# Fusing the four activation transposes of a pair of batches into one piece of a hand-ordered TensorE schedule

## The reference

```python
q = (layernorm(x) @ Wq)                    # 32 x 112 x 256 -> 16 heads of 64
k, v = split(ctx @ Wkv)                    # 32 x 375 x 192 -> 16 heads of 64
x = x + softmax(q k^T / 8) v @ Wproj + bproj
# FFN: 8 experts, top 2 of softmax(h @ gate_w), h = layernorm(x)
x = x + sum_over_top2(prob * (silu(h @ gate) * (h @ up)) @ down)
```

## Time and profile before

| what | value |
|---|---|
| median of three runs | 1473.92 us (1473.84 to 1474.1) |
| the profiled execution's time | 1469.35 us |
| its span | 1467.6 us |
| PE busy | 1426.4 us (97%), 11960 matmuls |
| PEld busy (weight loads) | 1264.4 us (86%) |
| DVE busy | 1054.7 us (72%) |
| ACT busy | 854.5 us (58%) |
| POOL busy | 624.9 us (43%) |
| mean granted TensorE clock | 0.994 |

### The profile page before, as it was taken

The page is one execution under the profiler, slowest core; times in us unless marked ns, Lnnn a source line. Parts: engine busy times, 40 slices in busy tenths (PEclk is TensorE's granted clock), DMA queues, the critical chain, the costliest instruction groups (busy, mean ns, idle before and its releaser), DMA issues.

```text
span 1467.6 us, 38599 instructions
## 1 busy us (share of the span) xinstructions
PE 1426.4 (97%) x11960; PEld 1264.4 (86%) x11961; DVE 1054.7 (72%) x2868; ACT 854.5 (58%) x2392; POOL 624.9 (43%) x671
## 2 busy tenths in 40 slices
PE   6999999999999999999999999999997999999996
PEld 5888889888888888888888898888886788888885
DVE  5667777777777777777777777777767776666664
ACT  5566556555665566656655656566555565555553
POOL 3634344344545343544344444545436243333332
PEclk9999999999999999999999999999999999999999
DMA  9322222222222232322222222212128243333232
GB/s 264 108 68 69 75 72 76 67 76 67 73 67 75 72 88 76 99 74 67 73 67 77 70 73 70 73 38 73 31 64 312 50 69 54 57 51 57 51 57 26
DMA packets 101508, 114.75 MB, mean 78 GB/s; under 512 B 17276, under 2 KB 88172, under 8 KB 101356
## 3 DMA queue, kind: packets, MB, share of 16 engines
q1 hardware_dynamic: 88300, 95.25, 22.3%
q0 software_dynamic: 12144, 15.66, 6.0%
q10 hardware_dynamic: 1024, 3.34, 0.7%
HBM read 62.28 MB, written 51.93 MB: 78 GB/s over the span
## 4 chain that ended last, share of the span: by engine, by line
PE 91%; DVE 3%; DMA 3%; issue 1%; ACT 0%; ACTq 0%; POOLq 0%; DVEq 0%; SPq 0%
PE bank L1486 26%; PE bank L1429 21%; PE bank L1555 11%; PE bank L1531 10%; PE bank L1521 9%; PE bank L1576 6%; PE bank L1493 4%; DMA out<-y_out,dest_now 2%; PE bank L1729 2%; DVE probT L1285 1%; PE bank L1682 1%; DVE Wgu L1138 1%; DMA WkU_whole<-in_L_xattn_Wkv 1%; DVE stat L1127 0%; DVE x L1125 0%
## 5 line engine op out<-in xcount | busy, mean ns | idle before, releaser
L891 ACT ACTIVATE prob<-bank,neg_max 112x375 f32<-112x375 f32 x512 | 300.4, 589 | 136.1 <-DVE neg_max L1279 136.1
L1279 DVE TENSOR_REDUCE neg_max<-bank 112x1 f32<-112x375 f32 x512 | 243.8, 539 | 16.4 <-PE bank L1521 16.3
L1531 PE MATMUL bank<-ident,prob 112*125 112x112 f32 x1536 | 213.8, 273 | 2.6 <-ACT prob L891 2.4
L1531 PEld LDWEIGHTS bank<-ident,prob 112*125 112x125 f32 x1536 | 198.3, 188 | 16.1 <-ACT prob L891 4.7
L1555 PEld LDWEIGHTS bank<-probT,V 125*64 125x64 f32 x3072 | 149.0, 137 | 39.7 <-issue 37.0
L822 POOL DMA_INDIRECT out<-y_out,dest_now x63 | 97.8, 1552 | 199.9 <-DMA out<-y_out,dest_now 139.8
L1046 DVE TENSOR_TENSOR K_l<-bank,K_h 128x376 fp32r<-128x376 f32 x256 | 140.3, 549 | 57.1 <-ACT K_h L847 52.7
L1555 PE MATMUL bank<-probT,V 125*64 125x112 f32 x3072 | 176.6, 264 | 3.3 <-DVE probT L1285 2.5
L1429 PE MATMUL bank<-Wgu,hT_h 128*128 x504 | 164.7, 408 | 3.4 <-DVE hT_l L1347 2.8
L845 ACT COPY V<-bank 125x512 f32<-125x512 f32 x96 | 56.4, 587 | 164.7 <-PE bank L1493 162.2
L847 ACT CAST K_h<-bank 128x376 fp32r<-128x376 f32 x256 | 121.0, 473 | 31.2 <-PE bank L1486 29.7
(11 more groups left out here) (217 smaller groups left out, 3962.1 us busy)
## 6 DMA issues: line engine op xcount, KB each, us to landing
bins<-pad_rows SPq DMA_DIRECT2D x29, 1032.0 KB, 6.0
inv_rows<-sums SPq DMA_DIRECT2D x126, 128.0 KB, 2.9
h_in<-bins SPq DMA_DIRECT2D x63, 129.0 KB, 2.2
Wgu<-in_L_ffn_gate_up_w SPq DMA_DIRECT2D x6, 1024.0 KB, 6.8
y_sb<-in_ctx SPq DMA_DIRECT2D x32, 187.5 KB, 2.7
y_sb<-in_ctx SPq DMA_DIRECT2D x62, 93.8 KB, 2.7
x_sb<-in_x SPq DMA_DIRECT2D x16, 224.0 KB, 2.9
x_res<-in_x SPq DMA_DIRECT2D x32, 112.0 KB, 2.5
```

Of the source, the lines that this page charges most:

```text
L891: nc.scalar.activation(prob[:, j, :], S_ps[j][0:LQ, 0:LKV], ACT.Exp, bias=neg_max[:, j:j + 1], accum_out=row_sum[:, head // HB, head % HB: ...
L1279: nc.vector.tensor_reduce(neg_max[:, j:j + 1], S_ps[j][0:LQ, 0:LKV], AX.X, ALU.max, negate=True).then_inc(max_done, 1)
L1531: last = nc.tensor.transpose(S_ps[j][0:KR, t * LQ:t * LQ + LQ], prob[:, j, t * KR:t * KR + KR], ident[0:LQ, 0:LQ])
```

## The change

`xT` becomes one piece with four transposes, which fill 448 columns of one bank, one cast of 448 columns and one subtraction of 448 columns. It stands in "early" of the even batch's step 3. In that batch's step 2, q 7 goes from "mid" (bank `A_ps[0]`) to "late" (bank `A_ps[1]`), where `xT` 0 had been, and "mid" is empty. The odd batch's step 2 keeps q 2 in "mid" and q 3 in "late". In `START` one `xT` piece takes the place of two; it waits for both rows of `xn`. GpSimd's wait before it overwrites `xn` names the one piece.

```diff
     q_at = {(1, 0): (0,), (1, 1): (1,), (1, 2): (2, 3), (1, 3): (4,), (0, 0): (5,), (0, 1): (6,), (0, 2): (7,)}.get((odd, s), ())
-    one = [("q", p) for p in q_at] + {(0, 2): [("xT", 0)], (0, 3): [("xT", 1)]}.get((odd, s), [])
+    one = [("q", p) for p in q_at] + {(0, 3): [("xT", 0)]}.get((odd, s), [])
     places = {"K": [("K", 2 * s), ("K", 2 * s + 1)],
               "early": one if s != 2 else [],
-              "mid": one[:1] if s == 2 else [],
+              "mid": one[:-1] if s == 2 else [],
...
-              "late": one[1:] if s == 2 else []}
+              "late": one[-1:] if s == 2 else []}
...
-    ("K", 0), ("xT", 0), ("xT", 1), ("K", 1), ("K", 2), ("K", 3), ("q", 0), ("q", 1), ("K", 4), ("K", 5), ("q", 2),
+    ("K", 0), ("xT", 0), ("K", 1), ("K", 2), ("K", 3), ("q", 0), ("q", 1), ("K", 4), ("K", 5), ("q", 2),
...
-                    pool.wait_ge(made, a.made(a.find(int(a.first), "xT", 1)))
+                    pool.wait_ge(made, a.made(a.find(int(a.first), "xT", 0)))
...
-                    nc.scalar.copy(xT_h[:, :, arg * LQ:arg * LQ + LQ],
-                                   src[:, 0:2 * LQ].rearrange("p (k q) -> p k q", k=2)).then_inc(hi_done, 1)
+                    nc.scalar.copy(xT_h[:].rearrange("p k q -> p (k q)"), src[:, 0:4 * LQ]).then_inc(hi_done, 1)
...
-                    lo, hi = xT_l[:, :, arg * LQ:arg * LQ + LQ], xT_h[:, :, arg * LQ:arg * LQ + LQ]
-                    ps = src[:, 0:2 * LQ].rearrange("p (k q) -> p k q", k=2)
+                    lo, hi = [t[:].rearrange("p k q -> p (k q)") for t in (xT_l, xT_h)]
+                    ps = src[:, 0:4 * LQ]
...
-                    pe.wait_ge(xn_done, 2 * (0 if a.first else pair + 1) + arg + 1)
-                    for t in range(2):
-                        last = nc.tensor.transpose(dst[:, t * LQ:t * LQ + LQ], xn[:, arg, t * P:t * P + P],
-                                                   ident[0:LQ, 0:LQ])
+                    pe.wait_ge(xn_done, 2 * (0 if a.first else pair + 1) + 2)
+                    for r in range(2):
+                        for t in range(2):
+                            last = nc.tensor.transpose(dst[:, (2 * t + r) * LQ:(2 * t + r) * LQ + LQ],
+                                                       xn[:, r, t * P:t * P + P], ident[0:LQ, 0:LQ])
                 elif kind == "q":
                     if arg == 0:
-                        pe.wait_ge(lo_done, a.split(a.find(1 if a.first else 0, "xT", 1)))
+                        pe.wait_ge(lo_done, a.split(a.find(1 if a.first else 0, "xT", 0)))
```

## The result

The kernel before took 1474.05 us in the median of 22 runs (1471.9 to 1477.17), the changed kernel 1476.68 us in the median of 22 (1473.98 to 1481.01). The ratio is 1.002, with a 95% interval of 1.0013 to 1.0027: slower, by about the 0.2% that the forecast named. Two further comparisons of the same two kernels gave 1.0025 (1.0014 to 1.0037) and 1.0017 (1.0008 to 1.0026). The medians lie 2.63, 3.98 and 3.03 us apart in the three.

The account below looks back on a forecast made before the run. TensorE holds 91% of the chain, so the waits ending last in steps 2 and 3 decide. 15 x 0.19 = 2.8, + 0.2 + 0.15 = +3.15 us on 1473.92 gives 1477.1 us; range 1474.0 to 1479.2.

Parts of the forecast that it names:

- Step 3's wide cast: Even batch's step 3: the 448-column cast delays head 3's exponential, which its transposes wait for; +0.19 us a pair.
- The cover of 0.19: Even step 3: the existing 0.19 us wait for head 1's exponential absorbs two more transposes (+0.20), leaving +0.01.
- Rival 1: Even step 3: the wider cast is hidden, only 0.01 a pair and 0.35 us remain; 1474.4 us, chance 0.13.
- Step 2's two transposes: Even batch's step 2: removing two transposes (0.20 us) gains 0, since `weigh` waits for VectorE's two copies.
- Rivals 2 and 3: VectorE doesn't hold step 2's `weigh`: with step 3's loss 1472.3 us, chance 0.07; without it 1469.5 us, chance 0.04.
- The wide subtraction: Even step 3: the 448-column subtraction ends before the second V piece needs the bank, margin 0.27 us; cost 0.
- Rival 4: Even step 3: the wide subtraction makes the second V piece wait; 1478.7 us, chance 0.14.
- q 7 to "late": Even step 2: the same six products moved later, ready before step 3's `scores` with margin 0.8 us; cost 0.
- Batch 0: Step 2 of the first batch, without `project`: q 7 delays `weigh`; +0.15 us once, bounds 0 and 0.2.
- Start: Before the first pair: one four-transpose piece waits for both rows of `xn`; +0.2 us, bounds 0 and +0.24.
- A pair of 69.2: Changed profile: one pair of batches lasts 69.2 us, against 69.03 before.
- The rule on grouping: Skill page: grouping pays on a saturated engine, splitting may help otherwise; ScalarE, 41.62 of 69.03 us busy, put under the second.

Follow-up runs that it names:

- a_third: The changed kernel, unaltered, profiled a third time: 1473.54 us against 1470.51 for the kernel before, ratio 1.0017.
- a_stats_late: The changed kernel with VectorE's statistics of the residual moved behind its two copies in step 2: 1467.84 us, ratio 0.9984 to the kernel before.
- b_again: The kernel before, unaltered, run once more for a second profile: 1477.52 us in one run.
- a_again: The changed kernel, unaltered, run once more: 1476.24 us against 1472.26 for the kernel before, ratio 1.0025.
- a_narrow_cast: The changed kernel with ScalarE casting only the first 224 of 448 `xT` columns within the pairs: 1474.43 us, ratio 1.0012 to the kernel before.
- a_narrow_sub: The changed kernel with VectorE subtracting only the first 224 of 448 `xT` columns within the pairs: 1473.66 us, ratio 1.0011 to the kernel before.
- b_late_sums: The kernel before plus one VectorE operation of 224 columns ahead of the even step 3's inverse sums: 1471.54 us against 1469.74, ratio 1.0009.
- b_third: The kernel before, unaltered, profiled a third time: 1472.65 us in one run.

## Why the prediction was right, step by step

**The sum.** Forecast +3.15, 1477.1 us. Measured 1476.68, a difference of the medians of 2.63 (0.13% to 0.27% by the interval). The mechanism is the one forecast, with a size for each term. That the sum came out so close is in part luck: the three comparisons scatter from 2.63 to 3.98, batch 0 cost 0.12 more than its term, and the term for the start can't be told from the spread of one kernel's starts.

**Step 3's wide cast, +0.19 a pair.** Right: 0.179, 0.184 and 0.191 in three profiles, gone with a narrow cast. The spacing of 0.41 is the forecast's. Head 3's loads follow head 2's after 0.74 and not 0.79: over the fourteen pairs of a_third head 3's come 0.19 later than before, measured from `weigh` of step 2, but head 2's come 0.04 later too, where the forecast had 0.01 for head 1 and nothing for head 2. The cover of 0.19 for the two additional transposes held too: with the narrow cast they cost -0.004. Rival 1 (the cast is hidden) falls.

**Step 2's two transposes, 0.** Right: -0.013 to 0.003. Rivals 2 and 3 said that VectorE isn't what holds `weigh`. a_stats_late shows that it is: with VectorE out of the way the same two transposes and the wait are worth 0.314, where the forecast's rows gave 0.32.

**The wide subtraction, 0.** Right: it ended 0.28 before the V piece needed the bank, 0.27 was forecast, and making it narrow left step 3 as it was. Rival 4 falls.

**q 7 to "late", 0.** Right within the pairs. **Batch 0, +0.15:** mis-sized. It was +0.27, beyond its bounds of 0 and 0.2. Appending q 7 to the end of the transposes was right: its first load comes 6.81 after step 1's `weigh` (46.84 to 53.65), the old kernel's `xT` loads came 6.81 after it too (46.37 to 53.18), and the six loads take the forecast's 0.67. What was too small is the step from q 7 to `weigh`: I had allowed 53.85 to 53.95, but `weigh` starts 0.20 later than q 7's own spacing would have it (0.31 instead of 0.11). The profile names no releaser for these 0.20, and their cause stays open.

**Start, +0.2:** not to be resolved. The first scores came at 30.81, 34.56 and 30.47 with the kernel before, at 31.29, 34.88 and 31.76 with the changed one. Taken two by two that is +0.48, +0.32 and +1.29, but the spread of one kernel is 4 us. Nearly all of that spread goes with the moment at which TensorE's pace doubles (last section). An estimate from the fourteen executions, a straight line by that moment with one step for the new order, puts the new order's start 0.19 later, give or take 0.15, which neither contradicts nor proves the term.

**A pair of 69.2:** right in a_third (69.226), 0.2 short in the first profile (69.436). The difference isn't the change's: b_again shows the same +0.21 with the kernel before. I had carried one profiled execution to the median as if executions differed by a constant; they differ in the pairs too.

**The rule on grouping.** The rows first: ScalarE was 60% busy, two casts made one left its busy time at 41.62, and TensorE lost 0.19 a pair. The Trainium skill's page "Perfetto Trace Analysis" (section "Optimizing Scalar/DVE Operations") advises to break up instructions of an engine that isn't saturated but makes others wait; by that rule the trace agrees with the forecast's side. The prediction's remark that the change would pay by the first half of the rule was a slip: that half speaks of a saturated engine, which ScalarE is not.

## What to carry to other kernels

Grouping two small operations of an engine that isn't the bound saved nothing here, and it moved the next instruction in that engine's queue back by the added columns (0.19 us for 224): put the grouped piece where that next instruction isn't what TensorE waits for. Before work is taken off the busiest engine, look at who ends the wait at the next meeting point; if it is another engine's queue, as here the statistics ahead of two copies, reorder that queue first, and the saving appears (0.314 a pair). And where two profiles of the same kernel haven't been compared, a difference of 0.2 us a pair may be the execution's.

## What the runs showed of the hardware

**A pause behind step 3.** In five of the fourteen profiled executions (the changed kernel's first, b_again, a_again, a_narrow_cast, a_narrow_sub) the signals of TensorE's products reach the other engines late in the even step 3. The signal of `weigh`'s last product comes 0.28 us after the product's start in the nine others, and 0.81 to 0.95 in four of these five (0.66 to 0.73 in a_narrow_sub), in each of the pairs 1 to 14. It is late in the odd step 3 as well (0.54 to 0.67), where the pair gets no longer by it: the remainder column is 0 or below but for 0.002 in a_narrow_sub. In the changed kernel's first profile no engine's signal arrives from 619.44 to 620.03. SP's issues and then GpSimd's indirect writes there:

```profile
617.52 0.60 SPq L523 DMA_DIRECT2D sums<-inv_sumT  x1
620.11 1.12 SPq L529 DMA_DIRECT2D inv_rows<-sums  x2
```

```profile
617.04 1.07 POOL L688 DMA_INDIRECT bins<-hn,bin_row  x1 [0.17 <-issue]
618.42 1.21 POOL L688 DMA_INDIRECT bins<-hn,bin_row  x1 [0.30 <-issue]
```

The second indirect write takes 1.21 here instead of 0.95, and the transfer's second part is issued 2.59 after the first, where it was 2.09 in the kernel before (613.35 to 615.44). Neither marks the effect: in b_again they are 0.96 and 2.09 and the V copy is late all the same, and a_third, without the effect, has a distance of 2.55 to 2.60 and two writes of 1.21 in its fourteen pairs. Price: 0.21 a pair with the kernel before, some 3 us of an execution. All four executions of the first comparison on one chip had it and none of the eight of the two later comparisons; a_narrow_sub has the late signal, but its V copy comes only 0.04 later, and its part is +0.038, no more than in the changed kernel without the effect (+0.049). What causes it stays open: late sums aren't needed for it (b_again) and don't bring it by themselves (a_third, b_late_sums), and moving the scatter couldn't test it.

**Matrix products at half pace at the start.** K products of 376 columns, the kernel before in its first execution, then in b_again:

```profile
17.13 0.52 PE L1466 MATMUL bank<-yB,WkU 128*128 128x376 f32 x1
17.44 0.45 PE L1486 MATMUL bank<-yA_h,WkH 128*128 128x376 f32 x1
17.72 0.33 PE L1486 MATMUL bank<-yA_l,WkH 128*128 128x376 f32 x1
17.89 0.34 PE L1486 MATMUL bank<-yA_h,WkL 128*128 128x376 f32 x1
```

```profile
21.65 0.52 PE L1486 MATMUL bank<-yA_h,WkL 128*128 128x376 f32 x1
21.96 0.52 PE L1486 MATMUL bank<-yB,WkT 128*128 128x376 f32 x1
```

They follow one another 0.31 apart until 17.4 in the one and until at least 21.96 in the other, then 0.17 apart. The view of busy time shows a granted clock of 1.00 on both sides of the switch, but the trace holds no record of the clock ahead of it: the first record, of the full clock, begins at 17.67 in the one and at 23.51 in the other, and the view counts time without a record as 1.00. The slow pace is that of a granted clock of 0.50, the level of 1.2 GHz: where a record shows 0.50, pairs of score products of 376 columns start 0.31 apart too (the kernel before, 1123.24 to 1123.55), and 0.17 once it shows 1.00 (1123.75 to 1123.92). Ahead of the late rise, in b_again, TensorE started no product from 15.77 to 17.43 and was busy from there on. Over all fourteen executions the first record begins between 16.98 and 23.51 and the first scores between 30.35 and 34.88, later with later (correlation 0.99), so most of the 4 us between starts goes with this moment.

**The granted clock at the transition.** Stretches of 4 us at the end of the first stage, of the kernel before and then of the changed one (the column ahead of the last two is the granted clock):

```profile
1120.00:1124.00 4.00, 3.92 (x36) 3.56 (x36) 2.06 (x11) 0.03 (x1) 3.53 (x5) 0.57 1.10 360
...
1136.00:1140.00 4.00, 2.69 (x12) 2.69 (x13) 3.79 (x3) 2.33 (x2) 1.26 (x1) 0.50 0.71 259
```

```profile
1120.00:1124.00 4.00, 4.00 (x36) 3.95 (x35) 2.47 (x6) 2.33 (x8) 0.03 (x1) 1.00 0.62 173
...
1140.00:1144.00 4.00, 2.66 (x12) 2.58 (x12) 3.33 (x2) 0.78 (x2) 1.28 (x1) 0.62 0.99 375
...
1148.00:1152.00 4.00, 3.86 (x11) 3.10 (x12) 3.90 (x6) 3.47 (x4) 0.00 (x0) 0.60 0.12 33
```

The clock falls to half, the level of 1.2 GHz, in different places of the same work; TensorE stood idle from 1132 to 1136 in the kernel before, and one of the falls lies in that stretch (0.73). The rest of the span moves by up to 3.6 us (404.54 to 408.16) with one kernel. That the clock does it isn't shown: the stretches at half clock around the transition add up to 10.2 us in the first execution of the kernel before and to 17.1 in b_third, but to 17.1 in b_again too, whose rest is 405.94.
